# Small experts beside the mixing layer: gate half's bank released on its own, three changes of order, and one load on another queue

## The reference, cut to what matters

```
# mixing branch, a linear recurrence over time, 16 heads of 4 keys and 8 values
r, k, v, g = xr @ W_r, xk @ W_k, xv @ W_v, xg @ W_g ;  decay = exp(-exp(w))
S = decay[..., None] * S + k[..., :, None] * v[..., None, :]     # scan over time
o = normalised(r . S + bonus) * gn_w + gn_b ;  out = (o * silu(g)) @ W_o
# expert branch: 64 small experts and a shared one, hidden width 64, 8 chosen per token
act = silu(x @ gate[e]) * (x @ up[e])
routed = sum over e of (act * router_mask[:, e]) @ down[e]
```

## Time and profile before

| | us |
|---|---|
| median of 3 runs | 4520.57 |
| lowest and highest | 4517.18, 4521.81 |
| the profiled execution, its own time | 4518.22 |
| its span, first to last instruction | 4516.4 |
| steps of the small experts, first to last matmul of `up_down` | 3738.2 to 4507.4 |
| PE, DVE, ACT, POOL busy over the whole span | 3959.8, 3338.1, 2924.7, 2333.6 |
| granted TensorE clock over the span | 0.953 |

### The profile page before, as it was taken

How to read it: one execution, slowest core, us unless ns; L and a number is a source line. 1 busy time by engine, 2 the same in 40 slices (tenths; PEclk the granted TensorE clock), 3 DMA queues, 4 the chain that set the end, 5 groups by cost and what they waited for, 6 DMA issues and landing times. The chain is left out here.

```text
span 4516.4 us, 87766 instructions
## 1 busy us (share of the span) xinstructions
PE 3959.8 (88%) x34522; PEld 2211.3 (49%) x34524; DVE 3338.1 (74%) x4661; ACT 2924.7 (65%) x4419; POOL 2333.6 (52%) x1475
## 2 busy tenths in 40 slices
PE   6999999999998989996877878897888868888898
PEld 3667666766766654451111211345777443333343
DVE  6888888888884557767889899466777746767676
ACT  2777777777776449963777777784565725544454
POOL 2888878888885013330221110371666536656665
PEclk7999999999999989996899999898999979999999
DMA  3212212221220011100110100231000325665554
GB/s 83 58 39 58 58 40 55 58 50 47 58 49 1 1 48 71 59 17 24 67 70 31 44 22 14 97 124 57 13 15 13 103 86 135 138 144 129 126 135 120
DMA packets 114056, 288.81 MB, mean 64 GB/s; under 512 B 24292, under 2 KB 36708, under 8 KB 111148
## 3 DMA queue, kind: packets, MB, share of 16 engines
q1 hardware_dynamic: 98228, 242.40, 20.7%
q0 software_dynamic: 15424, 40.89, 2.6%
HBM read 194.55 MB, written 52.91 MB: 55 GB/s over the span
## 5 line engine op out<-in xcount | busy, mean ns | idle before, releaser
L522 POOL TENSOR_TENSOR a_prob_low<-a_prob_whole,a_prob_high 128x1024 f16<-128x1024 f32 x512 | 1085.1, 2131 | 276.6 <-ACT a_prob_high L412 276.4
L496 DVE TENSOR_REDUCE a_part_max<-a_top 128x2 f32<-128x1024 f32 x512 | 626.1, 1223 | 218.8 <-PE a_top L323 212.9
L409 ACT ACTIVATE a_prob_whole<-a_score 128x1024 f32<-128x1024 f32 x512 | 525.2, 1026 | 332.5 <-PE a_score L312 320.6
L976 ACT ACTIVATE a_prob<-a_score 128x512 f32<-128x512 f32 x1024 | 533.0, 603 | 255.8 <-PE a_score L915 255.8
L1009 DVE TENSOR_REDUCE a_part_max<-a_side 128x2 f32<-128x1024 f32 x512 | 595.0, 1218 | 68.5 <-PE a_side L886 68.5
L412 ACT ACTIVATE a_prob_high<-a_score 128x1024 f16<-128x1024 f32 x512 | 521.8, 1019 | 0.0
L311 PE MATMUL a_score<-a_qa,a_ka 128*128 128x256 f16 x2048 | 476.3, 273 | 0.0
L312 PE MATMUL a_score<-a_qb,a_kb 128*128 128x256 f16 x2048 | 476.1, 273 | 0.0
L2210 POOL TENSOR_TENSOR m_lows<-m_scaled,m_high 128x512 f16<-128x512 f32 x264 | 325.8, 1239 | 257.2 <-ACT m_high L2164 257.1
L378 PE MATMUL a_o_ps<-a_v,a_prob_high 128*128 128x65 f16 x4096 | 428.7, 193 | 6.2 <-POOL a_prob_low L522 3.4
L380 PE MATMUL a_o_ps<-a_v,a_prob_high 128*128 128x64 f16 x4096 | 427.5, 194 | 0.0
(11 more groups left out here) (484 smaller groups left out, 10166.5 us busy)
## 6 DMA issues: line engine op xcount, KB each, us to landing
m_gate<-gates SPq DMA_DIRECT2D x264, 256.0 KB, 5.9
m_rep<-keys SPq DMA_DIRECT2D x8, 3072.0 KB
a_ka<-a_nat_high_k SPq DMA_DIRECT2D x128, 128.0 KB, 2.4
e_gate<-gates SPq DMA_DIRECT2D x8, 2048.0 KB, 7.2
slots<-in_slots SPq DMA_DIRECT2D x19, 520.0 KB, 4.2
a_qa<-a_nat_high_q SPq DMA_DIRECT2D x64, 128.0 KB, 2.4
a_qa<-a_nat_low_q SPq DMA_DIRECT2D x64, 128.0 KB, 2.4
a_qb<-a_nat_high_q SPq DMA_DIRECT2D x64, 128.0 KB, 2.4
```

What stands on the lines that cost most here:

```text
L409: eng.activation(prob_whole[:, e % RING, :, :, :], score[:, e % 2, :, :, :], ACT.Exp, scale=scale)
L496: eng.tensor_reduce(part_max[:, i, c, :, qt % 4], top[:, :, :], AX.X, ALU.max).then_inc(max_done, 1)
L522: eng.tensor_tensor(prob_low[:, e % RING, :, :, :], prob_whole[:, e % RING, :, :, :], prob_high[:, e % RING, :, :, :], ALU.subtract).then_ ...
L976: eng.activation(prob[:, e % RING, h, :], score[:, step % SLOTS, :], ACT.Exp).then_inc(exp_done, 1)
```

## The change

Five edits, all in `mixing_and_experts`:

1. `hidden_full` counts after the gate half's three matmuls, and a new semaphore `upper_full` after the up half's. PE's gate half waits for `weighted` (`acted` of two steps before), its up half for `upped`. DVE's `scaled` also waits for `upper_full`.
2. ACT does its mixing jobs last in the slot, behind silu and `high`.
3. DVE adds to the residual after `acted` and `scaled` of the slot.
4. The load of `rep` is issued by ACT, behind the silu of the slot, and no longer by SP.
5. It stands in slot 15 of the period (`SPREAD_AT`), before in slot 13.

```diff
-    KEEP_AT, SPREAD_AT = 12, 13
+    KEEP_AT, SPREAD_AT = 12, 15
...
+        upper_full = pl.sem("upper_full")
...
-                    c = (slot - SPREAD_AT) // PERIOD
-                    if (slot - SPREAD_AT) % PERIOD == 0 and c < CH:
-                        after_pe(eng, "o3", c - 1)
-                        eng.wait_ge(keys_out, 16 * (c + 1))
-                        eng.dma_start(rep[:, :, :], keys_d.rearrange("(h k) t -> h k t", k=GROUPS).unsqueeze(1).broadcast_to([16, 8, GROUPS, 3 * BANK])).then_inc(rep_in, 16)
...
                     if s >= HB:
+                        eng.wait_ge(weighted, s - HB + 1)
+                    x = [part[:, c * BANK:(c + 1) * BANK] for part in (x_high, x_low)]
+                    product(hidden[:, s % HB, :], 3 * j, n % 2, x, True, True).then_inc(hidden_full, 1)
+                    if s >= HB:
                         eng.wait_ge(upped, s - HB + 1)
-                    x = [part[:, c * BANK:(c + 1) * BANK] for part in (x_high, x_low)]
-                    product(hidden[:, s % HB, :], 3 * j, n % 2, x, True, True)
-                    product(upper[:, s % HB, :], 3 * j + 1, n % 2, x, True, True).then_inc(hidden_full, 1)
+                    product(upper[:, s % HB, :], 3 * j + 1, n % 2, x, True, True).then_inc(upper_full, 1)
...
-                    for name, c in act_jobs[slot]:
-                        mix(name, c)
...
                         eng.activation(hidden[:, s % HB, :], hidden[:, s % HB, :], ACT.Silu).then_inc(silu_done, 1)
                         if s % PER_UNIT == SPLIT_AT and s // PER_UNIT + 1 < UNITS:
                             split(s // PER_UNIT + 1)
+                    c = (slot - SPREAD_AT) // PERIOD
+                    if (slot - SPREAD_AT) % PERIOD == 0 and c < CH:
+                        after_pe(eng, "o3", c - 1)
+                        eng.wait_ge(keys_out, 16 * (c + 1))
+                        eng.dma_start(rep[:, :, :], keys_d.rearrange("(h k) t -> h k t", k=GROUPS).unsqueeze(1).broadcast_to([16, 8, GROUPS, 3 * BANK])).then_inc(rep_in, 16)
                     s = step_at(slot, HIGH_LAG)
...
                         eng.activation(high[:, s % HR, :], scaled[:, s % SR, :], ACT.Copy).then_inc(high_done, 1)
+                    for name, c in act_jobs[slot]:
+                        mix(name, c)
...
-                    s = step_at(slot, LAG + 1)
-                    if s >= 0 and s % J == J - 1:
-                        eng.wait_ge(out_used, s + 1)
-                        add_to_res(s % PER_UNIT // J, out[:, :], summed, s // J + 1)
                     s = step_at(slot, UP_LAG)
...
                         eng.wait_ge(weighted, s + 1)
+                        eng.wait_ge(upper_full, s + 1)
                         eng.tensor_tensor(scaled[:, s % SR, :], acted[:, :], upper[:, s % HB, :], ALU.mult).then_inc(upped, 1)
+                    s = step_at(slot, LAG + 1)
+                    if s >= 0 and s % J == J - 1:
+                        eng.wait_ge(out_used, s + 1)
+                        add_to_res(s % PER_UNIT // J, out[:, :], summed, s // J + 1)
```

## The result

| | us |
|---|---|
| changed kernel, median of 4 runs | 4592.26 (4586.95 to 4600.38) |
| kernel before, in the same runs | 4521.19 (4517.18 to 4522.72) |
| ratio, 95% interval | 1.016 (1.0142 to 1.0178) |
| profiled execution, own time and span | 4595.5, 4593.7 |
| granted clock over its span | 0.945 |

What follows compares the result with a forecast made beforehand. The prediction took PE as the bound, its waits being what can change. ACT's order +34, the load +18, bank and add -12 gave +40 us on 4518.2: 4558, as a median 4560; range 4512 to 4588.

Steps and rivals of the forecast that it cites:

- the lower clock: PE behind the new idle stretches: taken as no added cost, since they are shorter than the earlier stall of over 4 us.
- `mu2`'s wait, +19: Slot 4, chunks 1 to 7: `mu2` waits 2.7 us more for ACT's `std`, 7 times, +19 us.
- `r`'s wait, +15: Slot 10: `r` waits 2.2 us more for ACT's `kc`, 7 times, +15 us.
- Of ACT's other jobs none is waited for in its own slot.: ACT's remaining mixing jobs: the next user of the bank is one slot, over 2.8 us, further.
- at most 28: Upper end for the slow clock: two more idle stretches a period lose 2 us each, at most 28 us.
- The load, +18: `rep` competes with router weights by packets: 5.8 us worse in chunks 1, 5, 7, +1 in chunk 3, together +18 us.
- the rival by bytes: Queues share by bytes; router weights beside `rep` land within 16 us of first issue; 4510 as a median, faster; chance 0.12.
- in the even chunks `rep` starts no later: 0: Even chunks: `rep` was already queued behind the group before, and the next group again finishes last, so 0 us.
- The bank and the add, -12: Edits 1 and 3: 2 us in plain stretches, 10 us where DVE is late with its own jobs, together -12 us.
- ACT holding the issue of the load, hidden: Issuing `rep` holds ACT for 0.55 us, 8 times, hidden since ACT is busy 396 of 772 us.
- `kv01` not waiting: `kv01`, 9 slots later, first needs `rep`, which lands before the router weights that all wait for in any case.
- The rival "worse": The slow clock comes with the new waits (+28), or `kv01` does wait: 4580 to 4590; chance 0.15.

## Why the prediction was right or wrong

**Sign and the two new waits of `mu2` and `r`: right. Size: 40 forecast, 71 measured, 4 us above the range.** Two terms failed: the lower clock, put at nothing, and the stalls behind transfers, put at +18 and at nothing for edits 1 to 3. By PE's starts the four terms are +33, +21, +38.5 and -16, for +34, 0, +18 and -12 in the sum. Point by point:

- **`mu2`'s wait, +19.** 7 x 2.72 us = 19.0. Right, to the tenth of a microsecond.
- **`r`'s wait, +15.** 14.3 more than before. Right.
- **"Of ACT's other jobs none is waited for in its own slot."** Right in the changed kernel. With edit 2 without the others it is wrong in a small way: `ew` holds `out` of the chunk before for 0.56 us, and with `std` and `kc` first `v` comes to wait for the add, 1.1 us; that kernel is still +12.5 us. In the changed kernel PE has neither wait.
- **The lower clock, put at nothing. This is the first step that failed.** "I take 34, since these stretches are shorter than the one of rows 8": `mu2`'s wait of 2.7 us is enough here. In the changed kernel a stretch at 0.50 stands with each of the seven `mu2` waits, some 24 us in all, in which the matmuls lost 10 to 12 us, half of the 21 in the table above. The rest stands behind the longer stalls for transfers and behind a few other waits of 2.1 to 4.1 us for DVE and POOL. Alone edit 2 lost 27 us. It was my upper end, "at most 28": the term was seen and sized, and the wrong end of it taken. The 2 us that rows 1's stretch gave for one such place was fair (1.5 to 1.7 measured). The trace of the kernel before had already spoken against the step, in a place that the prediction does not use. PE's stall there at 4358.6 was 3.2 us by its starts, shorter than that of rows 8, and behind it the granted clock was 0.50 (the stall's row, then the columns of the earlier trace rows):

```profile
4358.59 0.39 PE L1971 MATMUL m_up_down<-m_x_high,m_w_high 128*128 128x512 f16 x1 [3.02 <-DVE m_scaled L2328]
...
4359.50:4362.50 3.00, 3.00 (x8) 0.90 (x7) 2.90 (x4) 1.12 (x2) 2.38 (x2) 0.50 0.71 164
```

- **The load, +18. The second one that failed.** PE's stalls behind transfers grew by 38.5 us in the profile. Only 19 of them go with edits 4 and 5 (82.2 for 63.3); the other 19.5 are there without them. The sum had no term for that: DVE reaches the same group earlier with edits 1 and 3 (+8 alone; in chunk 1 the group takes 17.9 us as before, and DVE waits 5.8 us for it in place of 4.3), and with edit 2 `rep` starts later against the group behind it (+8 alone). Alone edits 4 and 5 cost 25 us for the 18 forecast, a term of the right kind and too small. By packets was the right choice (the rival by bytes fell: 58 packets to 61, 1.43 MB to 0.25), but two numbers of the sum were short. In the odd chunks the group took 25.4 to 26.5 us and not 23.7, so DVE waited 12.9 to 14.1 and not 10.1. And "in the even chunks `rep` starts no later: 0" is false, as the issues in chunk 2 show, before and after:

```profile
3937.10 0.55 SPq L1943 DMA_DIRECT2D m_rep<-keys  x1
3947.97 3.69 SPq L1912 DMA_DIRECT2D m_gate<-gates  x6
```

```profile
3956.14 0.53 ACTq L2159 DMA_DIRECT2D m_rep<-keys  x1
```

  Before, `rep` had a start of 10.9 us over the next group. After, that group is issued at 3962.4 in this chunk, 6.3 us behind; DVE's waits in the even chunks went from 2.7 to 4.4 us up to 6.2 to 8.7. I had looked at the group ahead of `rep` and not at the distance to the one behind it. The Trainium skill, DMA: Bandwidth & Descriptors, section on queues, rings and completion order, says that an engine drains a whole packet of one ring before it turns to the next; the windows of packet counts agree, with packets of 24 KB beside 4 KB as well as with 6 KB ones, if the profile's packet is the page's. The page gives one as typically 9 to 17 descriptors, and no run here shows how many the profile's packets hold.
- **The bank and the add, -12.** By PE's starts the other waits fell by 16 in the whole, which holds every edit's effect on them, and by 12 with the pair alone. In time the pair is worth nothing, since the stalls behind transfers took 8 back and its executions spread too far to see the rest. What stood behind it was right in the plain stretch (the wait moves from `up_down` to `out`, 12.47 us becomes 12.43). What was missed is that the two edits are opposite: 14 us gained, 12 lost. I costed them together and so never asked what the first would give without the second.
- **ACT holding the issue of the load, hidden.** Right as far as seen: slot 13 from ACT costs nothing.
- **`kv01` not waiting.** Nearly: POOL waited for `rep` three times, 4.4 us in all, which counted for nothing beside 83.5 of the router weights.

The rival "worse", the lower clock with the new waits, 4580 to 4590, is the one that happened. Its clock cost 21 and not 28; the 4592 is above it because the stalls behind transfers had been put too low as well. The range's lower end does not follow from its own reason: 38 below 4560 is 4522, and 4512 was stated.

## What to carry to other kernels

Before a job is moved behind another in an in-order engine's slot, look for who needs it in that same slot and count the table loads between; here two jobs of 0.6 and 0.7 us cost 27 and 33 us. A transfer that is long and whose reader is far off must keep its distance to the short one behind it; a queue of its own does not replace that. And an edit that frees a buffer earlier is to be costed apart from one that reorders the engine behind it: together they showed nothing, alone they are -14 and +12. And a stall behind a transfer grows with every edit that brings the engine to it earlier or the transfer later, so it belongs in the sum of each.

## What was not expected of the hardware

PE's granted clock fell to 0.50 with waits of only 2.6 to 2.7 us in a stage where PE is otherwise busy, but not with each. In the changed kernel it did with all seven of `mu2`'s waits of 2.7 us and with none of the seven for `kc` of 2.6 us: after that of chunk 2 it was 1.00 from 3943 to 3946. With edit 2 alone it was 0.51 in the same place, and it fell with four of the seven for `kc` and six of the seven for `std` (3.4 us). There, and in the kernel with only `std` first (four of seven), PE had a wait of 0.56 us for `ew` shortly before that for `kc`; in the changed kernel and in the one without the load's move (one of seven) it had not. That the short wait before decides is a guess that no run tests. And two queues share the engines about one packet for one packet, at 24 KB against 4 KB as at 6 KB against 4 KB: the group's first part came in 17.8 us beside 24 KB packets and in 7.7 beside 6 KB ones, in the same slot.
